# A two-layer graph network on one core: the second layer gathers edge rows in nine shared tiles for a pair of units

## The reference

```python
h = maximum(layernorm(x), 0)
# first layer: messages with a softmax over the edges of one dst
c = concat([h[src], h[dst], relation[type]]) @ W1 + b1
b = leaky_relu(c @ w2, 0.01)
alpha = exp(b - segment_max(b, dst)[dst]) / segment_sum(...)[dst]
x = x + leaky_relu(segment_sum(c * alpha, dst), 0.01)
# second layer: plain sums of the neighbours' rows
h = maximum(layernorm(x), 0)
agg = segment_sum(h[src], dst)
x = x + where(deg > 0, agg, h)
```

## Time and profile before

| | us |
|---|---|
| median of 3 runs | 1948.25 (1937.6 to 1952.28) |
| the profiled execution's own time | 1953.42 |
| its span, first to last instruction | 1948.1 |
| busy in the span: PE, PEld, DVE, ACT, POOL | 1542.2, 1337.7, 1479.8, 1358.3, 1214.4 |
| mean granted TensorE clock | 0.889 |

### The profile page before, as it was taken

How to read it: one execution, slowest core, us unless ns; L and a number is a source line. 1 busy time by engine, 2 the same in 40 slices (tenths; PEclk the granted TensorE clock), 3 DMA queues, 4 the chain that set the end, 5 groups by cost and what they waited for, 6 DMA issues and landing times.

```text
span 1948.1 us, 35246 instructions
## 1 busy us (share of the span) xinstructions
PE 1542.2 (79%) x11747; PEld 1337.7 (69%) x11747; DVE 1479.8 (76%) x4127; ACT 1358.3 (70%) x3541; POOL 1214.4 (62%) x1042
## 2 busy tenths in 40 slices
PE   1389999999999999999998246767667587675778
PEld 0289999999999999999997134545445455453546
DVE  5469999999999999999988445756657476574757
ACT  0288888889888888888895335656657476574757
POOL 5757677777777777777710665565656666565550
PEclk9799999999999999999999668867878788787869
DMA  3545766666655666666545325655646556465544
GB/s 100 155 116 134 191 159 170 191 158 170 189 162 158 175 174 179 164 180 180 158 138 164 98 76 140 166 157 141 178 123 175 142 161 185 128 172 139 158 113 115
DMA packets 468073, 298.68 MB, mean 153 GB/s; under 512 B 34205, under 2 KB 436743, under 8 KB 467892
## 3 DMA queue, kind: packets, MB, share of 16 engines
q1 hardware_dynamic: 433876, 243.28, 46.0%
q0 software_dynamic: 34016, 53.16, 10.8%
HBM read 206.87 MB, written 104.34 MB: 160 GB/s over the span
## 4 chain that ended last, share of the span: by engine, by line
PE 45%; DVE 20%; another core or an unknown queue 13%; ACT 11%; issue 6%; POOL 1%; DMA 0%; SPq 0%; DVEq 0%; ACTq 0%; POOLq 0%
DVE st L1197 7%; PE c_p L1582 5%; PE t_p L1568 5%; PE c_p L1583 5%; ACT cs L1505 4%; DVE cs L1318 4%; PE c_p L1585 4%; PE t_p L1567 3%; DVE xn L1423 3%; ACT cs L1509 3%; PE y_p L1601 3%; PE y_p L1598 3%; PE t_p L1570 3%; PE y_p L1600 3%
## 5 line engine op out<-in xcount | busy, mean ns | idle before, releaser
L1093 POOL DMA_INDIRECT xe<-in_x,idx_t x516 | 690.5, 1338 | 245.0 <-issue 159.9
L1103 POOL DMA_INDIRECT xe<-x_d,idx x369 | 371.0, 1006 | 238.6 <-issue 140.5
L1505 ACT ACTIVATE cs<-xn,nbias,rstd 128x128 f32<-128x128 f32 x782 | 310.6, 479 | 272.3 <-remote 241.4
L1318 DVE TENSOR_SCALAR cs<-th,plc 128x256 f32<-128x256 f32 (+1 forms) x489 | 157.9, 388 | 264.0 <-remote 231.9
L1488 ACT ACTIVATE an<-xn,nbias,rstd 128x128 f32<-128x128 f32 x783 | 327.0, 484 | 1.0 <-issue 1.0
L1197 DVE BATCH_NORM_STATS2 st<-xn 128x6 f32<-128x256 f32 x855 | 314.5, 414 | 7.9 <-issue 6.4
L1491 ACT ACTIVATE ae<-xe,nbias,rstd 128x128 f32<-128x128 f32 x522 | 226.6, 483 | 0.0
L1582 PE MATMUL c_p<-w1a,th 128*128 128x129 f32 x1044 | 216.9, 289 | 9.4 <-issue 9.4
L1197 DVE BATCH_NORM_STATS2 st<-xe 128x6 f32<-128x256 f32 x482 | 186.2, 411 | 24.3 <-DMA xe<-x_d,idx 24.3
L1583 PE MATMUL c_p<-w1b,th 128*128 128x129 f32 x1044 | 203.8, 277 | 0.3
L1618 PE MATMUL y_p<-cs 128*128 128x128 f32 x792 | 131.0, 302 | 90.5 <-issue 85.7
(11 more groups left out here) (195 smaller groups left out, 3669.4 us busy)
## 6 DMA issues: line engine op xcount, KB each, us to landing
xn<-in_x SPq DMA_DIRECT2D x130, 384.0 KB
x_d<-xn SPq DMA_DIRECT2D x130, 384.0 KB
xn<-x_d SPq DMA_DIRECT2D x194, 256.0 KB
out<-xn SPq DMA_DIRECT2D x194, 256.0 KB
plr<-place_d SPq DMA_DIRECT2D x65, 256.0 KB
tyr<-types_d SPq DMA_DIRECT2D x65, 256.0 KB
xe<-in_x,idx_t POOLq DMA_INDIRECT x522
xe<-x_d,idx POOLq DMA_INDIRECT x369
```

The costliest lines, as they stand in the source:

```text
L1093: nc.gpsimd.indirect_dma_start(out=xe_of(u)[:, e, :], out_offset=None, in_=x, in_offset=bass.IndirectOffsetOnAxis(ap=idx_t[:, j:j + 1], ax ...
L1103: nc.gpsimd.indirect_dma_start(out=xe2_of(u)[:, k, :], out_offset=None, in_=x1_d, in_offset=bass.IndirectOffsetOnAxis(ap=idx2[:, j:j + 1], ...
L1318: last = v.tensor_scalar(sel2[:, u % 2, at:at + n], row2[:, 0:n], plc2[:, j:j + 1], None, ALU.is_equal)
L1505: a(own2_[:, u % 3, g, :], xs2_of(u)[:, g, :], ACT.Relu, bias=nbias[:, j % 2, c:c + 1], scale=rstd[:, j % 2, c:c + 1])
```

## The change

Two units (16 groups, UG2) share nine tiles. Tile 4 spans groups 6 to 9, so it belongs to both: the even unit gathers tiles 0 to 4, takes their statistics and normalises them, tile 4 into a buffer of its own (`shared2`, in `an`, which the first layer used); the odd unit gathers, measures and normalises only tiles 5 to 8, and multiplies tile 4 from shared2. Both have five selections and spans of 14 groups in all. The tables are kept per pair, 49 rows and nine rounds, which begin at T_WINDOW = 130 and are 15 steps apart (before: 150 and 22); the counts and borders are made 20 steps earlier. Gathers of the second layer: 440, before 489.

```diff
 UG = 8
-SPANS = ((0, 2), (1, 3), (3, 2), (4, 3), (6, 2))
-UT = len(SPANS)
+UG2 = 2 * UG
+SPANS = ((0, 2), (1, 3), (3, 3), (4, 4), (6, 4), (8, 4), (10, 3), (12, 3), (14, 2))
+PT = len(SPANS)
+UT = 5
...
-T_COUNT, T_CHAIN, T_WINDOW, T_APART = 60, 120, 150, 22
+T_COUNT, T_CHAIN, T_WINDOW, T_APART = 40, 100, 130, 15
...
-        row2 = th[:, 0, 0:3 * P]
+        row2 = th[:, 0, 0:4 * P]
...
             def tiles2(u):
-                return UT if u < NU2 - 1 else UT - 1
+                return UT - u % 2 - (u == NU2 - 1)
+
+            def spans2(u):
+
+                first = u % 2 * UG
+                found = []
+                for k in range(u % 2 * (UT - 1), u % 2 * (UT - 1) + UT - (u == NU2 - 1)):
+                    lo, hi = max(SPANS[k][0], first), min(SPANS[k][0] + SPANS[k][1], first + UG)
+                    found.append((k, lo - first, hi - lo, lo - SPANS[k][0]))
+                return found
...
# gather2
                     for k in range(tiles2(u)):
-                        j = NU2 * k + u
+                        j = NP2 * (u % 2 * UT + k) + u // 2
...
# POOL's loop over the first layer
-                    if (u - T_WINDOW) % T_APART == 0 and 0 <= (u - T_WINDOW) // T_APART < UT:
+                    if (u - T_WINDOW) % T_APART == 0 and 0 <= (u - T_WINDOW) // T_APART < PT:
                         window2((u - T_WINDOW) // T_APART)
                     gather(u)
...
-                pool.wait_ge(k_tables2, UT)
+                pool.wait_ge(k_tables2, PT)
...
+            shared2 = an[:, 0, 0:2, :]
...
# stats2
-                        if tiles2(u) == UT:
+                        if n == UT:
                             last = two_rows(j, c + UT - 1, xe2_of(u)[:, 0:UT:UT - 1, :])
...
# select2
-                    for k in range(tiles2(u)):
-                        j, n = NU2 * k + u, SPANS[k][1] * P
-                        last = v.tensor_scalar(sel2[:, u % 2, at:at + n], row2[:, 0:n], plc2[:, j:j + 1], None, ALU.is_equal)
+                    for k, first, n, c in spans2(u):
+                        j, n = NP2 * k + u // 2, n * P
+                        last = v.tensor_scalar(sel2[:, u % 2, at:at + n], row2[:, c * P:c * P + n], plc2[:, j:j + 1], None, ALU.is_equal)
                         at += n
...
# second_borders and second_tables: PT for UT and NP2 for NU2 throughout, UG2 for UG
...
# norm2
-                        last = a(edge2[:, u % 3, e, :], xe2_of(u)[:, e, :], ACT.Relu, bias=nbias[:, j % 2, c:c + 1],
-                                 scale=rstd[:, j % 2, c:c + 1])
+                        to = edge2[:, u % 3, e, :] if e < UT - 1 else shared2[:, u // 2 % 2, :]
+                        last = a(to, xe2_of(u)[:, e, :], ACT.Relu, bias=nbias[:, j % 2, c:c + 1], scale=rstd[:, j % 2, c:c + 1])
...
# aggregate2
-                    for k in range(tiles2(u)):
-                        first, n = SPANS[k]
+                    spans = spans2(u)
+                    ends = {g: i for i, (k, first, n, c) in enumerate(spans) for g in range(first, first + n)}
+                    for i, (k, first, n, c) in enumerate(spans):
+                        rows_ = shared2[:, u // 2 % 2, :] if k == UT - 1 else edge2[:, u % 3, k % UT, :]
                         for g in range(first, first + n):
                             if g < groups2(u):
-                                shared = k + 1 < tiles2(u) and g == SPANS[k + 1][0]
-                                last = mm(y[:, g // half, g % half * D:(g % half + 1) * D], sel2[:, u % 2, at:at + P], edge2[:, u % 3, k, :],
-                                          start=False, stop=not shared, skip_group_check=True)
+                                last = mm(y[:, g // half, g % half * D:(g % half + 1) * D], sel2[:, u % 2, at:at + P], rows_,
+                                          start=False, stop=ends[g] == i, skip_group_check=True)
                             at += P
```

More of the change, by code:

```diff
@@ L504, in gnn_two_layers @@
     NU2 = -(-GROUPS // UG)
+    NP2 = NU2 // 2
     NG2 = NU2 * UG
[L506 removed]
+    assert NU2 % 2 == 0 and XE2 % 2 == 0 and NP2 <= P and NG2 - 2 == GROUPS and NG2 - 2 == UN * NU - 1
+    assert SPANS[UT - 1][0] < UG < SPANS[UT - 1][0] + SPANS[UT - 1][1] and SPANS[UT - 2][0] + SPANS[UT - 2][1] <= UG <= SPANS[UT][0]
+    assert SPANS[PT - 1][0] >= UG2 - 2 and PT == 2 * UT - 1
     assert NU - (NQ - 1) * QU == 1 and P < REST < 2 * P
     tab_d = nc.dram_tensor("tab_d", (W, 3), f32, kind="Internal").ap()
[L511 removed]
+    borders_d = nc.dram_tensor("borders_d", (NG2 + UG2, 1), f32, kind="Internal").ap()
     scan_d = nc.dram_tensor("scan_d", (NU * UE, 4 * P), f32, kind="Internal").ap()
@@ L553, in gnn_two_layers @@
         less = spare2[0:TU, :].bitcast(bf16).rearrange("p (k s) -> p k s", s=SLOTS)
-        win2 = spare1[0:NU2, :].rearrange("p (c t) -> p c t", t=3)
-        pl2, skip2, idf2 = (spare2[0:NU2, k * P:(k + 1) * P] for k in range(3))
+        win2 = spare1[0:NP2, :].rearrange("p (c t) -> p c t", t=3)
+        pl2, skip2, idf2 = (spare2[0:NP2, k * P:(k + 1) * P] for k in range(3))
         idx_t = sb("idx_t", [P, UE * NU], u32)
@@ L1027, in load_ends2 @@
                 def load_ends2():
[L1028 to L1034, removed]
+                    by = borders_d.rearrange("(r j) o -> r (j o)", j=UG2)
+                    last = NP2 - 1
+                    sp.dma_start(ends2[0:last, 0:UG2], by[0:last, :]).then_inc(k_moved2, 16)
+                    sp.dma_start(ends2[0:last, UG2:UG2 + 1], by[1:NP2, 0:1], allow_slow_non_contiguous=True).then_inc(k_moved2, 16)
+                    sp.dma_start(ends2[last:NP2, 0:UG2 - 1], by[last:NP2, 0:UG2 - 1]).then_inc(k_moved2, 16)
+                    for c in (UG2 - 1, UG2):
+                        sp.dma_start(ends2[last:NP2, c:c + 1], by[last:NP2, UG2 - 2:UG2 - 1]).then_inc(k_moved2, 16)
                 sp.wait_ge(k_out, 32)
@@ L1121, in _ @@
                 pool.wait_ge(s_c, NU)
-                nc.gpsimd.iota(row2, pattern=[[1, 3 * P]], base=0, channel_multiplier=0, allow_small_or_imprecise_dtypes=True
+                nc.gpsimd.iota(row2, pattern=[[1, 4 * P]], base=0, channel_multiplier=0, allow_small_or_imprecise_dtypes=True
                                ).then_inc(k_row2, 1)
@@ L1352, in second_borders @@
                         b.mark(v.scalar_tensor_tensor(from2[:, k:k + 1], from2[:, k - 1:k], float(P), ends2[:, to:to + 1], ALU.add, ALU.min))
-                    if k == UT:
+                    if k == PT:
                         b.settle()
[L1355 to L1359, removed]
+                        v.tensor_copy(at2[:, :], from2[:, 0:PT]).then_inc(k_borders, 1)
+                        b.mark(v.tensor_scalar(from2[:, PT:PT + 1], from2[:, PT - 1:PT], float(P), None, ALU.add))
+                    if PT < k <= 2 * PT:
+                        i = k - PT
+                        at = SPANS[i][0] if i < PT else UG2
                         if i == 1:
@@ L1374, in second_tables @@
                     k, at = divmod(s - T_WINDOW, T_APART)
-                    if not 0 <= k < UT:
+                    if not 0 <= k < PT:
                         return
@@ L1624, in rows_to_tables2 @@
                     pe.wait_ge(k_rows2, k + 1)
-                    tr(b_p[:, 0:NU2], pl2, ident[0:NU2, 0:NU2])
-                    tr(b_p[:, P:P + NU2], idf2, ident[0:NU2, 0:NU2]).then_inc(k_rows2T, 1)
+                    tr(b_p[:, 0:NP2], pl2, ident[0:NP2, 0:NP2])
+                    tr(b_p[:, P:P + NP2], idf2, ident[0:NP2, 0:NP2]).then_inc(k_rows2T, 1)
                 def flag2_sum():
                     pe.wait_ge(k_borders, 3)
-                    mm(b_p[0:1, 2 * P:2 * P + 1], wrong2[:, UT:UT + 1], ones[0:NU2, :], start=True, stop=True).then_inc(k_flag2, 1)
+                    mm(b_p[0:1, 2 * P:2 * P + 1], wrong2[:, PT:PT + 1], ones[0:NP2, :], start=True, stop=True).then_inc(k_flag2, 1)
                 def scores_to_rows(k):
```

41 lines of the change are left out of this document (21 added, 20 removed).

## The result

The changed kernel takes 2016.7 us (median of 4, 2005.0 to 2032.1) against 1950.3 (4 runs, 1937.6 to 1952.5): ratio 1.036, interval 1.032 to 1.041. The forecast was 1889 and its range ended at 1932.

What follows compares the result with a forecast made beforehand. The second layer was taken as bound by cycles of POOL's unbroken gather runs plus 8.4 us. Terms -64 + 2 + 3 = -59 us took the profiled 1953.4 to 1894.4, less 5.2 for the median: 1889 us, range 1838 to 1932.

Steps and rivals of the forecast that it cites:

- Gathers, -64: Second layer: 49 fewer gathers shorten four-unit cycles from 34.41 to 31.80 us, -64 us; bounds -84 and 0.
- The law: Second layer: a cycle lasts its unbroken run of POOL gathers plus 8.4 us for recovery and a freed buffer.
- PE's two further matmuls: Second layer: two more matmuls a unit on PE, taken as 0, at most +44 us if all on the path.
- DVE and ACT: Second layer: wider selections against fewer statistics and normalisations; both engines end up no later, 0.
- Tables, +2: First layer: four more table rounds of short DVE and PE work, under 8 us on DVE, taken as +2 us.
- Tables, POOL's wait: First layer: POOL's window gather waits 16 us for the previous round, at eight rounds; +3 us, bounds 0 and 24.
- rival 3: First layer: unbroken catch-up gathers after each window wait slow PE, about 12 us a round; +37 us, 1985 us, chance 0.08.
- Rival 2: Second layer: half the cycles become the shorter, cheaper kind, about 7.4 us a unit; -105 us, 1843 us, chance 0.14.

Runs made afterwards that it cites:

- c1: The changed kernel itself, run again in a stalling group beside the kernel before: 2002.2 us, ratio 1.028.
- c2: The kernel before, unchanged, profiled once in a stalling group: second layer's first gather at 1081.5 us, then 861.2 us to the end of the span.
- c3: The changed kernel with POOL's window gathers nine positions later in its order, in a stalling group: 1904.8 us, ratio 0.978.
- f2: Changed kernel with windows nine positions later, plus five small waited-for memsets before each unit's second-layer gathers, in a quiet group: 1754.7 us, ratio 1.022.
- LATE = 9: The changed kernel with window gathers nine positions later in POOL's order: 1664.6 us (0.969) in a quiet group, 1904.8 us (0.978) in a stalling one.
- LATE = 2: The changed kernel with window gathers two positions later in POOL's order: 1666.6 us (0.971) in a quiet group, 1991.8 us (1.010) in a stalling one.

## Why the prediction was wrong, step by step

- **Gathers, -64**: right. -75.2 in the profiled execution, -63.8 between c1 and c2; 440 gathers; long cycles of 18 gathers, 32.0 us for 31.80; idle 8.04 for 8.42. The law (run of gathers plus recovery) held for such cycles, in the groups that stall; in the quiet ones there are no cycles, and POOL's issue is the bound of the stage: 49 gathers are worth 54 to 61 us.
- **PE's two further matmuls, 0 of up to 44**: right; the stage won no less than the gathers give. Likewise DVE and ACT. I had set against the row a rule of the Trainium skill ("DMA: Bandwidth & Descriptors", "Anatomy of one DMA": little time goes into making descriptors), by which fewer gathers would give nothing. These times don't fit that; what POOL does in its 1.00 us a gather the trace doesn't say.
- **Tables, +2**: too small; 10 to 18 us stay with the windows moved, in stalling groups, 4 in a quiet one. In the stalling group 13 us of them show as ACT's short waits (27.4 against 14.2 us).
- **Tables, POOL's wait, +3 with bounds 0 and 24**: the step that failed. The wait itself was right in place and nearly in size (20.2 us, said 16). Its price is 104.8 us of the first layer (c1 against c3), some 13 a round. I had priced it by one question, whether the first unit behind the window is late, and that was answered well: DVE waited 16.9 us in all for gathers from 500 us on. The other question, what the catch-up run does, I had put into rival 3 and taken out of the bounds.
- **Rival 3, 0.08, 1985**: this is what happened, with the announced sign, lone PE instructions before 1050 us. I had held it down with 29 gathers in a row at 1.79 us that harmed nothing. But the catch-up runs at 1.30, the pace of the second layer, whose runs do harm. 1.64 was the mean of the earlier trace rows, and a mean hid it: the median of those gathers is 1.11 us, the longest 3.68, and in the catch-up nearly all take 1.00. A chance of 8 in 100 for a mechanism that the same trace showed 25 times in the other stage was too low, and the range should have reached to it.
- **Rival 2's sum** has a slip: 98 units at 8.55 - 7.375 us less are -115 us, not -105. Nothing hangs on it.

The parts add up within one group: -63.8 (gathers), +18.2 (rounds), +104.8 (waits) are +59.2 us, and c1's profiled span is 59.2 us longer than c2's.

Nine places in POOL's order, for the window gathers alone, decided between 0.978 and 1.028. What I can't tell is why the same program stalls in one group of runs and not in another, nor what in the chip stalls. One rival is untested: the profile's page lists two DMA queues of kind "instruction", and the lone instructions with no wait in the profile would also fit a PE that gets its own instructions late while POOL fetches. No run here parts that from anything else.

The change with LATE = 9 beats the kernel before in both kinds of group, 0.969 and 0.978, and it beats the changed kernel in the group where both ran. LATE = 2 does as well where it is quiet (1666.6 us) and not where it stalls. In a stalling group breaks of 2.5 us each nine gathers make it 0.936; where they don't, such breaks cost about what they last (f2, 1.022).

## What to carry to other kernels

When a change makes a queue wait, price not only the first thing behind the wait but the whole catch-up: at which pace it runs, and whether the trace shows that pace doing harm in any other stage. A gather that waits for another engine's result may do as well later in its own queue, as it did here; look for the last position at which its reader is still in time. And when two pages of one kernel differ by 13% between groups of runs, compare only within a group, and look whether the change helps in both kinds.

## What the runs showed that I had not expected

- The kernel before took 1717 to 1718 us in two groups of runs and 1946 to 1973 in three. With late windows most of the difference is in the second layer, 618 against 804 us for the same 440 gathers; the first layer's part of it is 50 to 70.
- Pausing POOL made the kernel faster in a stalling group: some 108 us of added pauses (49 of 2.5 us in place of 0.3) took 86.6 us off the stage.
- A wait can come back by itself: the same code waits 11.85 us at the second window in both kinds of group, and then 5 us more in a quiet one and 94 more in a stalling one.
